# Last stage of a metaformer kernel: image 0's expert groups 2 and 3 weighted by bank and summed on GpSimd

## The reference, cut to what matters

```python
logits = jnp.einsum('bsd,de->bse', x, gate_w) + gate_b
probs = jax.nn.softmax(logits, axis=-1)
top_probs, top_idx = jax.lax.top_k(probs, 2)
top_probs = top_probs / jnp.sum(top_probs, axis=-1, keepdims=True)
dispatch = jnp.sum(jax.nn.one_hot(top_idx, n_experts, dtype=x.dtype) * top_probs[..., None], axis=-2)
h1 = jnp.einsum('bsd,edh->bseh', x, w1)
h2 = jnp.einsum('bsd,edh->bseh', x, w2)
hidden = jax.nn.silu(h1) * h2
expert_out = jnp.einsum('bseh,eho->bseo', hidden, w3)
return jnp.einsum('bseo,bse->bso', expert_out, dispatch)
```

## Time and profile before

| | |
|---|---|
| median of three runs | 309.79 us (308.72 to 310.91) |
| profiled execution, device time | 309.88 us |
| span, first to last instruction | 308.0 us |
| mean granted TensorE clock | 0.975 of full speed |
| TensorE matmuls busy | 267.9 us, 87% |
| VectorE busy | 237.0 us, 77% |
| ScalarE busy | 160.9 us, 52% |
| GpSimd busy | 128.9 us, 42% |

### The profile page before, as it was taken

The page is one execution under the profiler, slowest core; times in us unless marked ns, Lnnn a source line. Parts: engine busy times, 40 slices in busy tenths (PEclk is TensorE's granted clock), DMA queues, the critical chain, the costliest instruction groups (busy, mean ns, idle before and its releaser), DMA issues.

```text
span 308.0 us, 4965 instructions
## 1 busy us (share of the span) xinstructions
PE 267.9 (87%) x1719; PEld 136.2 (44%) x1730; DVE 237.0 (77%) x639; ACT 160.9 (52%) x353; POOL 128.9 (42%) x97
## 2 busy tenths in 40 slices
PE   8986869878987886998899889999999997999883
PEld 4332222222222233323455667865556754656551
DVE  2308999999999999797766885655878457898956
ACT  1138748846863353161557388767751556633431
POOL 4000898999999987743500044500001000003002
PEclk9999999999999999599999999999999799999998
DMA  6991000000000000003100000000000000000000
GB/s 180 328 399 65 0 2 1 1 2 0 1 2 0 0 2 0 0 2 128 78 0 2 1 3 0 2 2 1 2 1 0 3 0 2 0 0 3 0 11 9
DMA packets 5290, 9.50 MB, mean 31 GB/s; under 512 B 2721, under 2 KB 3425, under 8 KB 5010
## 3 DMA queue, kind: packets, MB, share of 16 engines
q1 hardware_dynamic: 5266, 9.19, 8.6%
HBM read 9.06 MB, written 0.13 MB: 30 GB/s over the span
## 4 chain that ended last, share of the span: by engine, by line
PE 41%; DVE 30%; POOL 12%; issue 9%; ACT 6%; POOLq 0%; DVEq 0%; ACTq 0%
DVE arena L1547 11%; POOL arena L503 7%; PE ps L1038 6%; PE ps L1053 6%; DVE arena L1538 3%; PE ps L848 3%; DVE x L1663 2%; PE ps L926 2%; PE ps L809 2%; PE ps L1210 2%; DVE arena L1889 2%; PE ps L1068 2%; PE ps L1197 2%; PE ps L815 2%; DVE arena L1663 2%
## 5 line engine op out<-in xcount | busy, mean ns | idle before, releaser
L503 POOL TENSOR_TENSOR arena<-arena 128x1024 f32<-128x1024 f32 x31 | 72.9, 2355 | 11.8 <-DVE arena L1547 9.2
L1547 DVE TENSOR_TENSOR_SCAN arena<-ps,arena 128x1024 f32<-128x1024 f32 x32 | 73.0, 2283 | 0.0
L626 ACT ACTIVATE ps<-ps,aneg 128x510 f32<-128x510 f32 x64 | 39.5, 656 | 47.4 <-PE ps L926 47.4
L448 POOL TENSOR_TENSOR rstd<-ve,mhalf 128x2 f32<-128x2 f32 (+1 forms) x14 | 10.4, 743 | 101.3 <-DVE ve L1419 93.9
L926 PE MATMUL ps<-arena 32*128 32x510 f32 x128 | 37.4, 668 | 15.0 <-DVE arena L1538 12.5
L1538 DVE TENSOR_TENSOR arena<-ps,arena 128x1024 f32<-128x1024 f32 x32 | 38.5, 1205 | 2.8 <-PE ps L932 2.7
L932 PE MATMUL ps<-arena 32*128 32x512 f32 x128 | 37.4, 667 | 0.7 <-DVE arena L1538 0.7
L685 ACT ACTIVATE arena<-ps,cols 128x256 f32<-128x256 f32 x64 | 25.6, 474 | 14.3 <-PE ps L1040 13.8
L970 PE MATMUL ps<-idle 128*128 128x512 bf16 x86 | 23.3, 386 | 1.1 <-issue 0.5
L1663 DVE SCALAR_TENSOR_TENSOR x<-ps,ww,x 128x64 f32<-128x64 f32 x86 | 18.0, 277 | 7.0 <-PE ps L1068 6.9
L926 PEld LDWEIGHTS ps<-arena 32*128 32x128 f32 x128 | 10.1, 190 | 28.6 <-DVE arena L1538 21.6
(11 more groups left out here) (232 smaller groups left out, 545.6 us busy)
## 6 DMA issues: line engine op xcount, KB each, us to landing
arena<-in_w SPq DMA_DIRECT2D x5, 512.0 KB, 5.3
bias<-in_rpb SPq DMA_DIRECT2D x1, 1408.0 KB, 7.4
w<-in_w SPq DMA_DIRECT2D x2, 512.0 KB, 5.6
arena<-in_w SPq DMA_DIRECT2D x1, 1024.0 KB, 11.0
arena<-in_w_conv SPq DMA_DIRECT2D x1, 576.0 KB, 4.0
w_bc<-in_w_bc SPq DMA_DIRECT2D x1, 512.0 KB, 6.2
c<-in_c SPq DMA_DIRECT2D x1, 336.0 KB, 5.6
arena<-in_spread SPq DMA_DIRECT2D x1, 256.0 KB, 6.4
```

The costliest lines, as they stand in the source:

```text
L503: pool.tensor_tensor(hc[:, i % HC_SLOTS], states[i % 4], c_all, ALU.mult).then_inc(hc_done, 1)
L626: act.activation(a, a, ACT.Exp, scale=aneg[:, q:q + 1]).then_inc(exp_done, 1)
L1547: dve.tensor_tensor_scan(h, decay_banks(i).rearrange("p s l -> p (s l)"), h, 0.0, ALU.mult, ALU.add).then_inc(scan_done, 1)
```

## The change

`add_fours(0)` now sums all four groups of image 0 on GpSimd: after `four[0]` += `four[1]` it waits for the fourth weighted group, adds `four[3]` to `four[2]` and then `four[2]` to `four[0]`, and then folds the halves. On VectorE `combine_four(0, 2)` and `combine_four(0, 3)` become `weighted_four(0, 2)` and `weighted_four(0, 3)`; `fours_added(0)` moves from ahead of `gate_mul(1, 1)` to behind `gate_mul(1, 5)`, and it is now what finishes image 0. `gate_mul(1, 3)` moves ahead of `router_second(3, 1)` and `gate_mul(1, 4)` ahead of `router_weights(3, 1)`. The counts of `comb`, `resid` and `acc_ready` follow: `four_turned(1, q)` waits on `comb` for every q, and `weighted_four(1, 0)` waits for `fours_added(0)`, which has read `four[0]`.

```diff
--- before.py
+++ after.py
@@ -535,9 +535,15 @@
 
             def add_fours(im):
 
-                pool.wait_ge(comb, 18 + 3 * im + 2)
+                base = 4 * im
+                pool.wait_ge(comb, 18 + base + 2)
                 pool.tensor_tensor(four[0], four[0], four[1], ALU.add).then_inc(acc_ready, 1)
-                pool.wait_ge(acc_ready, 2 * im + 1)
+                if im == 0:
+                    pool.wait_ge(comb, 18 + 4)
+                    pool.tensor_tensor(four[2], four[2], four[3], ALU.add).then_inc(acc_ready, 1)
+                    pool.wait_ge(acc_ready, 2)
+                    pool.tensor_tensor(four[0], four[0], four[2], ALU.add).then_inc(acc_ready, 1)
+                pool.wait_ge(acc_ready, base + (1 if im else 3))
                 v = four[0].rearrange("p (t e c) -> p t e c", t=TPI, e=4)
                 pool.tensor_tensor(v[:, :, 0:2], v[:, :, 0:2], v[:, :, 2:4], ALU.add).then_inc(acc_ready, 1)
 
@@ -1326,14 +1332,12 @@
             def four_turned(im, q):
 
                 pe.wait_ge(yb_act, 12 + 4 * im + q + 1)
-                if im == 1 and q == 1:
-                    pe.wait_ge(resid, len(NORMS) + 1)
-                elif im == 1 and q >= 2:
-                    pe.wait_ge(comb, 21 + q - 1)
+                if im == 1:
+                    pe.wait_ge(comb, 21 + q)
                 elif q == 3:
                     pe.wait_ge(logits_read, 8)
                 else:
-                    pe.wait_ge(comb, 18 + 3 * im + q)
+                    pe.wait_ge(comb, 18 + q)
                 if q == 0 and im == 0:
                     pe.wait_ge(logits_read, 7)
                 for t in range(TPI):
@@ -1894,6 +1898,8 @@
                 stage = 6 + im
                 n = LN_OF_FFN[3]
                 dve.wait_ge(y_turned, 24 + 4 * im + q + 1)
+                if im and q == 0:
+                    dve.wait_ge(resid, len(NORMS) + 1)
                 o = E_OF[3] * TPI * im
                 w = tiles(ww[:, o:o + E_OF[3] * TPI], TPI)[:, :, 4 * q:4 * q + 4].unsqueeze(3).to_broadcast([P, TPI, 4, CH])
                 dve.tensor_tensor(four[q].rearrange("p (t e c) -> p t e c", t=TPI, e=4),
@@ -1904,13 +1910,17 @@
                 n = LN_OF_FFN[3]
                 tt = slice(TPI * im, TPI * im + TPI)
                 v = four[0].rearrange("p (t e c) -> p t e c", t=TPI, e=4)
-                dve.wait_ge(acc_ready, 2 * im + 2)
+                dve.wait_ge(acc_ready, 2 * im + 4)
                 settle()
                 if im:
-                    dve.wait_ge(comb, 24)
+                    dve.wait_ge(comb, 25)
                 link(dve.tensor_tensor(x[:, n + 1, tt], x[:, n + im, tt], v[:, :, 0], ALU.add))
-                mark(dve.tensor_tensor(x[:, n + 1, tt], x[:, n + 1, tt], v[:, :, 1], ALU.add))
-                added[:] = [(dve_step, steps[0])] * TPI
+                last = dve.tensor_tensor(x[:, n + 1, tt], x[:, n + 1, tt], v[:, :, 1], ALU.add)
+                if im == 0:
+                    last.then_inc(resid, 1)
+                else:
+                    mark(last)
+                    added[:] = [(dve_step, steps[0])] * TPI
 
             def combine_four(im, q):
 
@@ -1919,7 +1929,7 @@
                 dve.wait_ge(y_turned, 24 + 4 * im + q + 1)
                 src = bank(four_bank(im, q)).rearrange("p (t e c) -> p t e c", t=TPI, e=4)
                 for e in range(4):
-                    done = (comb, 18 + 3 * im + 3) if q < 3 else (resid, len(NORMS) + 1 + im)
+                    done = (comb, 18 + 4 + 3) if q < 3 else (resid, len(NORMS) + 1 + im)
                     weigh(3, im, src[:, :, e], 4 * q + e, x[:, n + 1, tt], im == 1 and q == 2 and e == 0, e == 3, done)
 
             gate_mul(0, 0)
@@ -1945,16 +1955,16 @@
             turned(7)
             router_top(3, 1)
             gate_mul(1, 0)
+            gate_mul(1, 1)
+            weighted_four(0, 2)
+            gate_mul(1, 2)
+            weighted_four(0, 3)
+            gate_mul(1, 3)
+            router_second(3, 1)
+            gate_mul(1, 4)
+            router_weights(3, 1)
+            gate_mul(1, 5)
             fours_added(0)
-            gate_mul(1, 1)
-            combine_four(0, 2)
-            gate_mul(1, 2)
-            combine_four(0, 3)
-            router_second(3, 1)
-            gate_mul(1, 3)
-            router_weights(3, 1)
-            for j in range(4, 6):
-                gate_mul(1, j)
             weighted_four(1, 0)
             gate_mul(1, 6)
             gate_mul(1, 7)
```

## The result

The changed kernel has a median of 307.45 us over 20 runs (305.81 to 309.25), the kernel before 309.84 us over 20 runs (305.67 to 311.24). This ratio leaves out, as slow, runs over 1.5% above the fastest of their kernel (seven of the kernel before, all above 310.7 us, and none of the changed one), and the medians of all 20 runs differ by more, 2.39 us or 0.8%.

A forecast was written before the change was run, and what follows sets the result against it. The prediction took TensorE's wait for gate_mul(1, 3) as the bound: a ceiling of 1.96 us, cut by GpSimd's hold on VectorE to 1.19, so 309.79 - 1.19 = 308.6 us, range 307.0 to 310.1.

The forecast's parts named there:

- TensorE's hole: Last stage, 291.4 to 293.3 us: TensorE does nothing while gates(1, 5) waits for VectorE's gate_mul(1, 3).
- Rival 1: Last stage: GpSimd's hold on VectorE costs little or nothing; 1.89 to 1.96 us gained, 307.9 us; chance 0.3.
- the price of the hold: VectorE's router_second stretched by GpSimd's sums, delaying later products; gain 1.19 us instead of 1.96.
- the signs named: Last-stage profile: idle gap at 291.4 gone, gates(1, 5) near 291.3, three router_second instructions stretched, tail 1.2 us earlier.
- The bound: Last stage: TensorE's idle 291.4 to 293.3 us is what can be won, closed by an earlier gate_mul(1, 3).
- VectorE's list up to `gate_mul(1, 3)`: VectorE, last stage: new order with weighted_four puts gate_mul(1, 3) at 290.27 to 290.95 us.
- The ceiling of 1.96: TensorE: gates(1, 5) can start at 291.34 instead of 293.30, at most 1.96 us gained, with 1.07 us per step.
- I take B as first: GpSimd's second sum at 291.76 starts ahead of VectorE's L1624 at 291.78, so L1624 is held until 293.08.
- the rule in the prediction: VectorE instructions with two SBUF inputs contend with SBUF-reading GpSimd ones; whoever is first keeps the ports for its whole instruction.
- What the hold delays: TensorE: gates(1, 6) starts 0.41 us late, and down_four(1, 2), needing gate_mul(1, 5), at 296.08 instead of 297.27.
- L1595 set free: VectorE's L1595 no longer held by GpSimd's fold: 0.44 us given back, worth nothing as gate_mul(1, 1) waits for its silu.
- The waits: VectorE's fours_added(0) waits for GpSimd's fold, ending at 293.83; VectorE comes there later, so the wait is free.

The follow-up runs named there:

- e1_order: Kernel before with only gate_mul(1, 3) moved ahead of router_second and gate_mul(1, 4) ahead of router_weights; 15.07 us to gate_mul(1, 7), ratio 0.9981.
- e3_full_order: Kernel before with gate_mul(1, 3) moved ahead of combine_four(0, 3) and gate_mul(1, 4) right behind it; 13.81 us to gate_mul(1, 7), ratio 0.9948.
- e4_early: Changed kernel with router_second(3, 1) moved up behind gate_mul(1, 0); 13.83 us to gate_mul(1, 7), ratio 0.9951.
- e2_bank: Changed kernel with gate_mul(1, 3) back behind router_second and gate_mul(1, 4) behind router_weights; 16.53 us to gate_mul(1, 7), ratio 1.0007.
- e5_pool_late: Changed kernel with GpSimd's three sums for image 0 waiting until gate_mul(1, 5) is done; 15.6 us to gate_mul(1, 7), 306.05 us in one run.

## Why the prediction was right, and where it was off

The direction held, and so did the mechanism of the gain: TensorE's hole was the bound and the early `gate_mul(1, 3)` closed it. The size did not: forecast were 1.19 us and 308.6, measured 2.21 us in the last stage and a median of 307.45. Rival 1 is what happened. The step that failed is the price of the hold, 1.96 - 1.19 = 0.77 us, which turned out as nothing. That 307.45 lies in the range of 307.0 to 310.1 proves little, since that range is 3.1 us wide and would have held no gain at all too. Of the signs named, the hole is gone and `gates(1, 5)` moved; two of the three instructions were stretched, as rival 1 says; and the parts ahead of the last stage differ by 0.45 us, less than the gain.

1. *The bound.* Right. `gates(1, 5)` waited for `gate_mul(1, 3)`; e1_order and e3_full_order moved only products and got 0.91 and 2.17 us. That the chain from there belongs to TensorE is shown by the same two and by e4_early, where `router_second` was free of the hold and nothing moved.
2. *VectorE's list up to `gate_mul(1, 3)`.* Right to 0.01: forecast at 290.27, measured at 289.81 + 0.45 = 290.26.
3. *The ceiling of 1.96.* Too low by 0.25. I took 1.07 us for a step of eight matmuls from a row in which the next step was a `down_four`; measured were 0.97 and 0.96 for the two steps behind the former hole, so 0.10 twice. The saving belongs to two steps that follow each other directly, and the trace of before already had such a pair, 0.96 us apart, where the second step's first matmul is also shorter:

```profile
287.24 0.48 PE L1309 MATMUL ps<-xt,arena 64*128 64x256 f32 x1
...
288.20 0.42 PE L1309 MATMUL ps<-xt,arena 64*128 64x256 f32 x1
```

`gates(1, 4)` also started 0.05 earlier (289.77 + 0.45 = 290.22), since `gate_mul(1, 2)` was ready earlier.
4. *The hold.* The mechanism was right, and the Trainium skill's rule ("SBUF — State Buffer", Who interferes with whom) agrees with L1627, L1630 and e2_bank's L1628. Its price was wrong in one step: "I take B as first". L1628 came 0.01 us behind the start of the second sum and still went first, so one sum held one instruction fewer. This is a single instance; in e2_bank an instruction that started 0.05 behind a sum was held. The same section of the Trainium skill also names tensor_scalar among the instructions that can take the shared ports; e4_early's L1646 agrees. I had counted only instructions with two inputs. Nor does every GpSimd instruction that reads SBUF hold them, as the rule in the prediction would have it: a `pow` of 128 x 2 did not, and the measurement decides. In e1_order three VectorE instructions with two SBUF inputs ran inside it, each at its usual length of 0.18 or 0.19; one of them and the `pow`:

```profile
279.04 0.18 DVE L1645 TENSOR_TENSOR wr<-oh,wc 128x32 f32<-128x32 f32 x1
```

```profile
278.84 0.70 POOL L448 TENSOR_TENSOR rstd<-ve,mhalf 128x2 f32<-128x2 f32 x1 [6.40 <-DVE ve L1419]
```

5. *What the hold delays.* I let `down_four(1, 2)` wait for `gate_mul(1, 5)`. It started at 294.60, while that product ran from 294.15 to 294.84: its first four matmuls need only `gate_mul(1, 4)`, and the wait stands ahead of the fifth. Rival 1's 1.89, plus the 0.25 of point 3, plus the 0.07 by which I had delayed `down_four`, is 2.21.
6. *L1595 set free.* Right, 0.45 us of VectorE, and worth nothing: VectorE then stood idle for 0.94 us ahead of `gate_mul(1, 1)`.
7. *The waits.* The fold ended at 293.46, `fours_added(0)` came at 294.76 after VectorE's own queue, without idle time. e5_pool_late shows what it would have cost otherwise.

How much of the gain is order, and how much the work taken off VectorE, the prediction did not separate. With the changed kernel's order but the old `combine_four` (e1_order) 0.91 of the 2.21 us came; in the changed kernel the other 1.30, by difference, are owed to the shorter list ahead of `gate_mul(1, 3)`. That less work is neither enough nor needed: in the old order it made the stage 0.55 us longer (e2_bank), and with the product moved one place further ahead 2.17 us came without it (e3_full_order).

## What to carry to other kernels

When one engine stands idle for a product of another, first ask whether that product can stand further ahead in the other's list: here two moved lines (e3_full_order) gave what a rewrite of the sum gave. Additions that are given to GpSimd aren't free for VectorE: look at which VectorE instructions run beside them, and keep those with two SBUF inputs, or SBUF-to-SBUF tensor_scalars, away from the path meanwhile. Whether a hold is hidden depends on the order: with `router_second` behind `gate_mul(1, 3)` it cost nothing, and with `router_second` ahead of it the stage was 0.55 us longer than in the old kernel.

## What the runs showed of the hardware that wasn't expected

The runs of one kernel fall in groups: the changed kernel's 20 lie at 305.8 to 306.3, at 307.1 to 307.5 and at 308.9 to 309.3 us. Two places ahead of the last stage can be seen in which profiles differ though their programs do the same there; that these make the groups is not shown. The first is at the start, where the same 128 x 512 matmul (L840; one in the program, recorded as two) took 2.04 us in the profile of before and 1.10 in that of e3_full_order:

```profile
8.67 2.04 PE L840 MATMUL ps<-xt,arena 128*128 128x512 f32 x2 [0.76 <-DVE xt L1440]
```

```profile
7.70 1.10 PE L840 MATMUL ps<-xt,arena 128*128 128x512 f32 x2 [0.76 <-DVE xt L1440]
```

The scan's first product came at 30.93 us in the one and at 28.10 in the other. The granted clock is shown as 1.00 in both from 7 to 9 us, so the rows leave the cause open. The second is a dip of the granted clock from 244 to 246 us, 0.84 in the profile of before and 1.00 in that of the changed kernel (columns as in the earlier trace rows):

```profile
244.00:246.00 2.00, 2.00 (x16) 1.05 (x14) 0.84 (x4) 1.57 (x4) 0.29 (x1) 0.84 0.00 0
```

```profile
244.00:246.00 2.00, 2.00 (x16) 1.12 (x18) 0.84 (x4) 1.75 (x5) 0.52 (x1) 1.00 0.01 4
```

Between a GpSimd instruction at 243.60 and the one at 258.56 the kernel before took 14.96 us, the changed kernel (243.82 to 258.12) 14.30, though nothing differs there in the program. TensorE was busy for 14.17 us of the one and 13.48 of the other, so it is its busy time that grew; the mean granted clock was 0.97 and 1.00. A difference of one or two us between two single profiles of this kernel says nothing; an interval between two instructions near the change does.
